# Two normalised convolutions on one NeuronCore: where the second image half's moves, the 7th and 8th bands and the third image's statistics stand in the start-up

## The reference, cut to what matters

```python
def _gn(v, G=16, eps=1e-05):
    B_, C_, H_, W_ = v.shape
    g = v.reshape(B_, G, C_ // G, H_, W_)
    m = jnp.mean(g, axis=(2, 3, 4), keepdims=True)
    s = jnp.var(g, axis=(2, 3, 4), keepdims=True)
    return ((g - m) / jnp.sqrt(s + eps)).reshape(v.shape)

x = x + _L0_conv_ref(_gn(x), L0_conv_weight, L0_conv_threshold)   # 3x3, padding 1, weights masked by a threshold
x = x + _L1_conv_ref(_gn(x), L1_conv_kernel, L1_conv_bias)        # 5x5 (written as an FFT), padding 2, with bias
return x
```

## Time and profile before

| | |
|---|---|
| median of three timed executions | 805.59 us (803.62 to 805.67) |
| the profiled execution's own time | 804.16 us |
| its span, first to last instruction | 802.4 us |
| TensorE (PE) busy | 748.6 us, 93% of the span |
| VectorE (DVE) busy | 607.1 us, 76% |
| ScalarE (ACT) busy | 332.5 us, 41% |
| GpSimd (POOL) busy | 266.9 us, 33% |
| moved by DMA | 150.49 MB, mean 188 GB/s |
| mean granted TensorE clock | 0.990 |

### The profile page before, as it was taken

The page is one execution under the profiler, slowest core; times in us unless marked ns, Lnnn a source line. Parts: engine busy times, 40 slices in busy tenths (PEclk is TensorE's granted clock), DMA queues, the critical chain, the costliest instruction groups (busy, mean ns, idle before and its releaser), DMA issues.

```text
span 802.4 us, 67796 instructions
## 1 busy us (share of the span) xinstructions
PE 748.6 (93%) x32292; PEld 529.2 (66%) x32292; DVE 607.1 (76%) x959; ACT 332.5 (41%) x287; POOL 266.9 (33%) x161
## 2 busy tenths in 40 slices
PE   0885799999999999999999999999999999999996
PEld 0442487776776767677676867677676767676553
DVE  6986687796878787897878788797878796764541
ACT  0450335363534434363534335363444426361410
POOL 1104044443223343432224343432234343322360
PEclk9998899999999999999999999999999999999999
DMA  8899589999999979798998979798998956573424
GB/s 199 186 194 219 114 183 234 222 222 221 227 226 222 222 176 223 171 222 198 220 206 203 225 168 226 182 223 198 225 209 207 194 131 163 131 167 87 102 52 105
DMA packets 234176, 150.49 MB, mean 188 GB/s; under 512 B 18656, under 2 KB 227616, under 8 KB 230048
## 3 DMA queue, kind: packets, MB, share of 16 engines
q1 hardware_dynamic: 227168, 144.00, 81.8%
q10 hardware_dynamic: 6272, 4.90, 2.6%
q0 software_dynamic: 704, 1.25, 0.7%
HBM read 75.60 MB, written 33.59 MB: 136 GB/s over the span
## 4 chain that ended last, share of the span: by engine, by line
PE 90%; DVE 3%; issue 2%; DMA 1%; ACT 1%; DVEq 1%; SPq 1%; ACTq 0%
PE psum L892 68%; PE psum L909 22%; DMA x_bands<-x_dram 1%; DVE bn_in L640 1%; DVE x_lo L742 1%; SPq L269 1%; DVE mid L762 0%; DVEq L805 0%; DVEq L765 0%; ACT conv_out L486 0%; ACT x_bands L454 0%; ACT x_hi L409 0%; DVE x_bands L714 0%; DVE mid L873 0%; DVEq L59 0%
## 5 line engine op out<-in xcount | busy, mean ns | idle before, releaser
L385 POOL TENSOR_TENSOR mid<-mid,conv_out 128x512 f32<-128x512 f32 x118 | 243.6, 2094 | 457.8 <-ACT conv_out L486 457.8
L892 PE MATMUL psum<-x_hi,s_hi 32*64 32x508 f16 (+2 forms) x6656 | 197.9, 379 | 10.3 <-ACTq L526 4.8
L892 PE MATMUL psum<-x_hi,s_lo 32*64 32x508 f16 (+2 forms) x6656 | 198.3, 379 | 5.2 <-issue 5.2
L892 PE MATMUL psum<-x_lo,s_hi 32*64 32x508 f16 (+2 forms) x6656 | 197.8, 378 | 4.3 <-DVE x_lo L742 2.4
L892 PEld LDWEIGHTS psum<-x_hi,s_hi 32*64 32x64 f16 x6656 | 123.4, 104 | 73.9 <-ACTq L526 6.3
L892 PEld LDWEIGHTS psum<-x_hi,s_lo 32*64 32x64 f16 x6656 | 133.6, 104 | 56.7 <-issue 7.4
L892 PEld LDWEIGHTS psum<-x_lo,s_hi 32*64 32x64 f16 x6656 | 107.3, 104 | 80.4 <-issue 10.6
L762 DVE SCALAR_TENSOR_TENSOR mid<-psum,unscale,x_own 128x1024 f32<-128x1024 f32 x64 | 79.2, 1279 | 89.1 <-PE psum L909 89.0
L409 ACT ACTIVATE x_hi<-x_bands 128x2304 f16<-128x2304 f32 x31 | 65.7, 2119 | 116.0 <-PE psum L909 115.9
L486 ACT ACTIVATE conv_out<-psum,bias,unscale 128x512 f32<-128x512 f32 x118 | 82.4, 776 | 60.8 <-PE psum L892 60.8
L750 DVE TENSOR_TENSOR x_lo<-mid_bands,x_hi 128x2560 f16<-128x2560 f32 x32 | 92.5, 2891 | 2.8 <-PE psum L892 2.7
(11 more groups left out here) (88 smaller groups left out, 341.4 us busy)
## 6 DMA issues: line engine op xcount, KB each, us to landing
x_own<-x_dram SPq DMA_DIRECT2D x128, 256.0 KB, 4.8
mid_bands<-mid SPq DMA_DIRECT2D x372, 80.0 KB, 3.1
out_dram<-mid SPq DMA_DIRECT2D x112, 256.0 KB, 5.5
x_bands<-x_dram SPq DMA_DIRECT2D x96, 288.0 KB, 5.8
x_bands<-x_dram SPq DMA_DIRECT2D x32, 272.0 KB, 7.0
mid_bands<-mid SPq DMA_DIRECT2D x124, 64.0 KB, 2.7
every_mv<-mv_scratch ACTq DMA_DIRECT2D x16, 256.0 KB, 3.8
out_dram<-mid SPq DMA_DIRECT2D x28, 128.0 KB, 2.4
```

The lines of the kernel that those rows point to most:

```text
L385: nc.gpsimd.tensor_tensor(m, m, conv_out[:, b, :], ALU.add).then_inc(out_added, 1)
L892: ins = nc.tensor.matmul(psum[2 * C * J:2 * C * (J + 1), bank + i, :].rearrange("p (a w) -> p a w", a=A)[:, :, c0:c1], w[quad(i), at:at + ...
```

## The change

Four edits. (1) GpSimd's sixteen moves of half 1 of mid wait for `mv_in` (the first exchange has landed) instead of for bands 5. (2) On SP, bands 6 wait until all sixteen of those moves have landed; the first DMA of bands 7 follows, and the other three wait until the second load of slot 0, which is bands 6, has landed; SP's own wait for `mv_in` ahead of `move_mid(2)` goes away, since `mid1_moved` comes after it. (3) On ScalarE, in step 3 only, `high3(4)` goes ahead of `normalize5(1)`. (4) On VectorE, the statistics of bands 4 and 5 and their aggregate go ahead of `normalize5_first` and `low5(0)`.

```diff
@@ sync
             load_bands(5)
             move_edges(0, 0, 1)
             load_own(3)
+            sp.wait_ge(mid1_moved, 16 * Q * Q)
             load_bands(6)
-            load_bands(7)
-            sp.wait_ge(mv_in, 16)
+            load_bands(7, x_bands_in[0], 2 * Q)
             move_mid(2)
@@ gpsimd
             pool.wait_ge(mid_made, PIECES * 2)
-            pool.wait_ge(x_bands_in[5], 16 * Q)
+            pool.wait_ge(mv_in, 16)
             for i in range(Q):
@@ scalar
                     high5_first()
+                elif s == LAG:
+                    high3(s + 1)
+                    normalize5(1)
+                    high5(1)
                 else:
@@ vector
             low3(LAG)
-            normalize5_first()
-            low5(0)
             stats_in(4, range(BANKS))
             stats_in(5, range(BANKS))
             aggregate("x", 2, mv_ready)
+            normalize5_first()
+            low5(0)
             stats_out(2)
             dve.wait_ge(mv_in, 16)
```

## The result

The changed kernel takes 813.06 us (median of five, 811.77 to 814.18), the kernel before in the same comparison 804.40 us: a ratio of 1.0104, 95% interval 1.0088 to 1.0120, so 8.7 us slower. The forecast was slower by 2.6, with 806 to 811 as its own range. The profiled execution took 814.18 us, 10.0 more than the one of before; its span is 812.3 us against 802.4, and its whole start-up before step 3 lies 1.3 us later.

What follows compares the result with a forecast made beforehand. PE was taken as the bound, fed after start-up, so start-up gaps count fully. Of -9.5 us from gaps all is lost to late bands and +2.6 remains: 805.59 + 2.6 = 808.2 us, own range 806 to 811.

Steps and rivals of the forecast that it cites:

- The first exchange and the held moves: Start-up: statistics told at 68.1, exchange in at 75.0 (11.9 us earlier), GpSimd's moves all landed at 86.7.
- the second rival: Moves or exchange stay slow, holding bands may win nothing for the write: 817.5 or 816.0 us, chance 0.13.
- PE's gaps: PE's first pass through whole_step: five distances at 3.75 us each, last piece at 89.3 instead of 98.73, -9.5 us.
- the other end: PE's first pass with distances of 4.49 us: last piece at 93.0, only -5.8 us.
- the sum: At step 6 the -9.5 us of PE's gaps is lost again to late bands, and +2.6 remains.
- SP's lateness: SP through bands 6 and 7 in 8.3 us, at 95.0; move_mid(2) ends at 105.4 instead of 99.63: 5.7 us late.
- the 4.7 us of the earlier trace: SP's wait for bands 6 behind three fresh DMAs, from two waits of 12.1 us in all, the longest 7.4.
- What hangs on bands 9: Statistics 5.7 us late, less 2.0 of cover: 3.7 late; low3(6) gives +1.8, the exchange of step 5 gives +2.6.
- +2.6: Net loss in us at PE's pairs5_high(4), by way of the exchange of step 5; forecast 808.2 us, chance 0.50.
- The path in step 7: take_conv5(3) ends at 176.9 instead of 173.48; with 0.1 us for the drain, PE's pairs5_high(4) starts 2.6 late.
- The first rival's condition: Rival that the gain is kept in part, chance 0.22: holds if SP's lateness at bands 9 is below about 3 us.
- the 3.5 us of gain: First rival's size: second exchange 2.3 us earlier, PE 3.5 us earlier at pairs5_high(2) in step 5, giving 802.1 us.

Runs made afterwards that it cites:

- the kernel without the chain: The change, but bands 7 do not wait for bands 6: 806.93 us, ratio 1.0030 to the kernel before.
- SP made late: The kernel before, but SP waits ahead of own rows 5 until ScalarE's high5(2) is done: 811.89 us, ratio 1.0099.
- bands 9 ahead of the store: The change, but SP issues bands 9 ahead of the first output store: 812.38 us, ratio 1.0109 to the kernel before.
- the kernels without GpSimd's hold or without SP's tie to it: Kernels whose GpSimd moves start at bands 5 as before (the change so altered: 803.10 us) or whose SP does not wait for those moves (805.81, 803.40).
- the two whose rows stand above: The change with GpSimd's moves not held and bands 7 not waiting for bands 6 (803.84 us); half 2's moves ahead of the bands, GpSimd's moves not held (805.26).
- the interleaved order: VectorE's and ScalarE's orders changed, GpSimd's moves at bands 5, one DMA of bands 6 and 7 behind every second move of half 2: 799.53 us, ratio 0.9942.
- SP's alone: The kernel before with only SP's edit, GpSimd's moves still starting at bands 5: 803.41 us, ratio 0.9994.
- the kernel with GpSimd's but not SP's: The change with SP as before, all other edits kept: 805.81 us, ratio 1.0026 to the kernel before.
- the kernel with neither hold nor chain: The change, but GpSimd's moves start at bands 5 and bands 7 do not wait for bands 6: 803.84 us, ratio 1.0001.

## Why the prediction was right in its mechanism and wrong in its size

- **The first exchange and the held moves: right.** Told at 67.9, in at 74.2, moves landed at 86.7; all within 1 us of the forecast. The 2 KB write took 2.3 us until the read could be issued in the change (67.93 to 70.21), and 12.1 where bands 6 and 7 were in flight (69.01 to 81.10), so the part of the second rival by which holding them wins nothing fell. The turn-taking of queues in the Trainium skill ("DMA: Bandwidth & Descriptors", "Queues, rings and completion order"), by which that write should not have waited, is not borne out by these two rows.
- **PE's gaps: 6.0 us won at the last piece, not 9.5, and 4.4 at the end of the pass.** The distances are 3.5 to 5.9 us, near the 4.49 that stood as the other end; the clock behind the last gap, which the sum left out, took 1.6 back. It made no difference, since all of it was lost behind, as were the 9.4 in the kernel without the chain.
- **SP's lateness is the term that was mis-sized: 5.7 forecast, 9.3 measured.** Three pieces of the list took longer: bands 6 and 7 10.1 us instead of 8.3, because the wait for bands 6, measured at 6.7, was put at the 4.7 us of the earlier trace rows, a place where the first of the four awaited DMAs was long done (here all four were fresh); own rows 4 and the edges 6.1 instead of 4.8 (107.66 to 113.75, where the kernel before had 99.67 to 104.46); `move_mid(2)` 10.7 instead of 10.35. Together 3.5. What SP waited for is this row of the chain after the change:

```profile
88.04 7.56 DMA x_bands<-x_dram
```

  The experiment without the chain, which takes 5.4 us from SP at this place and 6.1 from the time, agrees with a price of nearly one to one.
- **What hangs on bands 9: the second term that was mis-sized.** The 2.0 us of cover at `take_conv3(5)` held. The exchange of step 5 was forecast to shift as it is; it also grew: from 145.78, when the aggregates ended, to 158.39 before, and from 153.28 to 168.68 after, 15.4 us instead of 12.6. DVE before, then after (the earlier trace rows has neither; 168.68 stands above):

```profile
145.47 0.31 DVE L650 BATCH_NORM_AGGREGATE mv<-bn_in 128x2 f32<-128x48 f32 x1
...
158.39 0.40 DVE L685 SCALAR_TENSOR_TENSOR product<-every_mv,mix_in 128x128 f32<-128x128 f32 x1 [4.88 <-DMA every_mv<-mv_scratch]
```

```profile
152.97 0.31 DVE L654 BATCH_NORM_AGGREGATE mv<-bn_in 128x2 f32<-128x48 f32 x1
```

  Why it grew stays open. Its write fell at the end of an output store before (141.60 to 146.18 on SP) and into the middle of one after (150.85 to 155.01), but over all fourteen kernels the same exchange took 9.8 to 15.4 us: 13.9 with SP made late, 10.3 with bands 9 ahead of the store. With 3.8 from SP's list (the exchange starts 7.5 late, forecast 3.7) and 2.8 from this exchange, +2.6 becomes +9.2, against the 9.9 of the trace.
- **The path in step 7 was nearly right, and the clock stood nowhere in it.** `take_conv5(3)` ends at 183.68, and 0.1 for the drain gives 9.4 us at `pairs5_high(4)`, where the forecast had PE wait. PE starts there 0.5 later still and without a wait. It had waited 2.26 us for `high3(7)`, which hangs on the same exchange, and behind that wait the granted clock was on average 0.59 from 178 to 182 us, part of that time at the lower of its two levels (1.00 before, 174 to 178): the 48 matmuls of `pairs3_high(7)` with the high weights took 2.79 us instead of 1.53. The forecast put this at nothing ("From there on PE runs as before").
- **"At +2.6 it holds whatever PE won": right**: PE was 4.4 us ahead in the change, 9.4 without the chain and not at all in the kernel before with SP made late, and each ended later than the kernel before.
- **The first rival's condition** (lateness below 3 us at bands 9) was met in the kernels without GpSimd's hold or without SP's tie to it, and there the loss is gone or down to 1.6 us; without the chain it was just met (2.8 late), and 2.8 us stay lost. But the 3.5 us of gain that it priced came in none of them: in the two whose rows stand above, the bands ran beside PE's first pass and lengthened it, or came too late for the second exchange. That trade was missing in the forecast; only the interleaved order escaped it, with 5.1 us.

## What to carry to other kernels

A wait put into an engine's instruction list is charged to everything behind it in that list, and two waits in a row (here SP for GpSimd, GpSimd for the exchange) add up to 8.7 us, though here SP's alone cost nothing that could be measured and the kernel with GpSimd's but not SP's lost 1.6. Before holding work back, look for the first place behind it where an engine already waits for a later item of the same list (here VectorE for bands 9). The only cover there is the time that this engine then still waits for something else (here 2.0 us for PE). Where bulk loads and short transfers that others wait for shared DMA, interleaving small and large transfers won 0.6% in this kernel, where holding and pulling forward won nothing.

## What the runs showed of the hardware

PE's first pass through the loop body stops for its program. The DMA view of the kernel before has a queue of its own for instructions, q8, with three reads from 60 to 86 us and three from 86 to 103 (queue, count, MB, share of 16 engines):

```profile
q8 instruction: 3, 0.05, 1.0%
```

```profile
q8 instruction: 3, 0.05, 1.4%
```

From 103 us to the end there is one more. In slices of 1 us the reads begin in those from 59, 67, 76, 83, 87, 91 and 95 us, and a piece of PE's work begins about 3 us behind each (62.92 to 98.73); in the second pass there are neither reads nor gaps. How far apart the pieces lie went with what else DMA carried: 3.5 to 4.9 us in the change from 70.45 to 86.85 us, with GpSimd's moves in flight but no bands, 5.9 for the last piece, when bands 6 and 7 had started to move, and 7.3 to 9.0 in the kernel before with these bands in flight. In the kernel with neither hold nor chain, where the bands followed at 78 us, 7.2 us of idle time lie ahead of one piece.

A write of 2 KB on ACT's queue, timed until the read that waited for it could be issued, took 2.0 to 2.6 us in five kernels where neither bands 6 and 7 nor GpSimd's moves were being issued, 3.7 to 4.2 in five with GpSimd's moves, and 10.5 to 13.2 in four with bands 6 and 7 in flight, of which one had no moves of GpSimd beside them (12.1).

Behind some of its waits PE ran at the lower of its clock's two levels for a while: in the change the granted clock was on average 0.67 from 150 to 154 us, behind a wait of 3.42 us, and 48 matmuls took 2.81 us there, where the kernel before has 1.00 in the same 4 us and 1.52 for these matmuls.
